# TensorE's order inside one step of a linear-attention and feed-forward kernel: four small-matmul groups and two big ones change places

## The reference

```python
xx = shifted(x) - x;  xk, xv, xr, xg = x + xx * time_maa_{k,v,r,g}
r, k, v = xr @ Wr.T, xk @ Wk.T, xv @ Wv.T          # per head
g = silu(xg @ Wg.T)
def step(state, inp):                              # one chunk of 64 tokens
    att = rc @ kc * w_mat                          # the scores, weighed
    yc = att @ vc + rc @ state * wb                # products with V, products with the state
    new_state = ws * state + kc * wk @ vc          # the state update
out = (normalized(y) * gamma + beta) * g @ Wo.T    # the output projection
x = x + out
x = x + gelu(layernorm(x) @ W0.T + bias0) @ W1.T + bias1
```

## Time and profile before

| | |
|---|---|
| median of three runs | 2102.96 us (2094.62 to 2105.97) |
| the profiled execution | 2098.03 us, its span 2096.2 us |
| TensorE matmuls | 2009.1 us busy, 27206 of them, and as many weight loads |
| VectorE | 1739.2 us busy |
| ScalarE | 1292.4 us busy |
| GpSimd | 317.8 us busy |
| mean granted clock of TensorE | 0.988 of full speed |

### The profile page before, as it was taken

How to read it: one execution, slowest core, us unless ns; L and a number is a source line. 1 busy time by engine, 2 the same in 40 slices (tenths; PEclk the granted TensorE clock), 3 DMA queues, 4 the chain that set the end, 5 groups by cost and what they waited for, 6 DMA issues and landing times.

```text
span 2096.2 us, 64752 instructions
## 1 busy us (share of the span) xinstructions
PE 2009.1 (96%) x27206; PEld 1432.4 (68%) x27206; DVE 1739.2 (83%) x3687; ACT 1292.4 (62%) x2081; POOL 317.8 (15%) x329
## 2 busy tenths in 40 slices
PE   5889999999999999999999999999999999999999
PEld 4777666676766766766766776766776666767666
DVE  7788888888888988888988887888888888888761
ACT  7776565676655667655657765666765656776442
POOL 1011110111111111111111111111111101111110
PEclk8999999999999999999999999999999999999999
DMA  6977786788776788777778877778887867887767
GB/s 212 211 204 237 186 235 211 233 247 237 205 232 200 235 239 237 212 225 215 232 223 242 245 207 210 233 218 245 247 237 192 229 200 244 247 237 205 217 231 254
DMA packets 428979, 471.97 MB, mean 225 GB/s; under 512 B 259600, under 2 KB 309392, under 8 KB 428688
## 3 DMA queue, kind: packets, MB, share of 16 engines
q1 hardware_dynamic: 427056, 467.64, 76.6%
q10 hardware_dynamic: 1632, 0.18, 0.1%
HBM read 316.21 MB, written 25.17 MB: 163 GB/s over the span
## 4 chain that ended last, share of the span: by engine, by line
PE 77%; SPq 5%; DVE 4%; issue 4%; ACT 4%; DMA 4%; POOL 0%; ACTq 0%; DVEq 0%
PE F L1132 19%; PE F L1068 15%; PE B L879 9%; PE B L1040 8%; PE sc L879 7%; PE YT L911 5%; PE YT L879 3%; DMA y<-ygT 3%; PE YT L963 2%; SPq L2026 2%; PE sc L941 2%; PE YT L982 2%; PE F L836 1%; PE YT L1012 1%; SPq L2013 1%
## 5 line engine op out<-in xcount | busy, mean ns | idle before, releaser
L1068 PE MATMUL F<-xT,ring 128*128 128x256 f16 x3840 | 459.0, 276 | 16.6 <-issue 12.1
L1132 PE MATMUL F<-ring,hT 128*128 128x512 f16 x1984 | 467.5, 379 | 0.0
L1068 PEld LDWEIGHTS F<-xT,ring 128*128 128x128 f16 x3840 | 374.0, 99 | 81.4 <-issue 20.3
L1132 PEld LDWEIGHTS F<-ring,hT 128*128 128x128 f16 x1984 | 189.1, 98 | 197.8 <-issue 0.3
L1767 ACT ACTIVATE hT<-F,b,f_rho 128x256 f16<-128x256 f32 x480 | 244.2, 561 | 102.0 <-PE F L1068 102.0
L879 PE MATMUL B<-mix,WT 128*128 128x256 f16 x2304 | 267.5, 273 | 0.1
L879 PEld LDWEIGHTS B<-mix,WT 128*128 128x128 f16 x2304 | 222.6, 98 | 33.4 <-DVE gT L1371 0.3
L276 DVE SCALAR_TENSOR_TENSOR mixf<-dx,maa,xnT 128x256 f32<-128x256 f32 x512 | 238.6, 527 | 0.1
L1724 ACT ACTIVATE Shl<-S 128x256 f16<-128x256 f32 x128 | 53.4, 417 | 257.4 <-PE YT L982 140.4
L1970 POOL TENSOR_TENSOR Shl<-S,Shl 128x256 f16<-128x256 f32 x128 | 89.4, 698 | 756.9 <-ACT Shl L1724 756.9
L1338 DVE TENSOR_TENSOR att<-att 128x512 f16<-128x512 f32 x256 | 166.8, 693 | 39.2 <-ACT att L1718 39.0
(11 more groups left out here) (196 smaller groups left out, 2998.6 us busy)
## 6 DMA issues: line engine op xcount, KB each, us to landing
ring<-w_dram SPq DMA_DIRECT2D x512, 512.0 KB, 4.6
kx<-kT SPq DMA_DIRECT2D x96, 256.0 KB, 3.8
rx<-rT SPq DMA_DIRECT2D x96, 256.0 KB, 4.4
xa<-in_L_attn_x SPq DMA_DIRECT2D x32, 512.0 KB, 7.7
vbd<-vN SPq DMA_DIRECT2D x256, 64.0 KB
x<-in_L_attn_x SPq DMA_DIRECT2D x32, 512.0 KB, 6.3
out<-x SPq DMA_DIRECT2D x31, 512.0 KB, 3.8
w_dram<-ring SPq DMA_DIRECT2D x20, 256.0 KB, 3.5
```

What stands on the lines that cost most here:

```text
L1068: mm = eng.matmul(up_place(f, j)[:, i * BT:(i + 1) * BT], ring[:, use % RING, i, a * C + kk * P:a * C + (kk + 1) * P], xT[:, :, kk, :], st ...
L1132: mm = eng.matmul(F[:, t, :], hT[:, k, rows(t)], ring[:, use % RING, i, a * C:(a + 1) * C], start=(k == 0 and a == 0), stop=(k == NH - 1 a ...
```

## The change

Only TensorE's list changes. The eighth up piece moves from behind the third scores to between the products with V and those with the state; the first half of the output projection moves to right behind the products with the state; then come the third scores and the second tile's state update, which before stood behind the first down piece. The rest of the step stays. No matmul, no semaphore and no wait is added or dropped.

```diff
         if att_n:
             pe_att_v(eng, n, 0)
-            pe_from_state(eng, n, 0)
-            pe_scores(eng, n, 2)
-            pe_prepare(eng, n, "sc2")
         if ff:
             pe_up(eng, n, 7)
+        if att_n:
+            pe_from_state(eng, n, 0)
         if tail:
             pe_Wo(eng, n, 0)
+        if att_n:
+            pe_scores(eng, n, 2)
+            pe_kv(eng, n, 1, n < STEADY)
+            pe_prepare(eng, n, "sc2")
+        if tail:
             pe_prepare(eng, n, "Wo0")
         if ff:
             pe_down(eng, n - 2, 0)
         if att_n:
-            pe_kv(eng, n, 1, n < STEADY)
             pe_scores(eng, n, 3)
```

## The result

| | before | after |
|---|---|---|
| median of seven runs each | 2104.80 us (2094.62 to 2109.18) | 2088.64 us (2083.68 to 2091.96) |
| ratio after to before | | 0.9926, 95% interval 0.9905 to 0.9948 |
| the profiled execution, its span | 2098.03, 2096.2 us | 2091.96, 2090.2 us |
| TensorE on "issue", 250 to 2010 us | 36.5 us in 14 pauses | 10.9 us in 17 pauses |
| undisturbed steps apart | 59.94 us | 60.92 us |

The change makes the kernel 0.7% faster. The two profiled executions differ by only 6.1 us, the medians by 16: that of before (2098.03) was 7 us faster than the median of its kernel, that of after (2091.96) is the slowest of its seven runs.

The account below looks back on a forecast made before the run. TensorE, busy 2009.1 of 2096.2 us, bounds the kernel; pauses and low clock cost 51.8. Span 2096.2 - 43.6 won + 29.2 switches and VectorE wait + 2 late weights = 2083.8; forecast 2086 us, range 2062 to 2107.

Parts of the forecast that it names:

- The pauses are refills of 256 instructions: TensorE's "issue" pauses at the small matmuls: 256 instructions running in less than a refill's 4 to 6 us can stop it.
- What is left is 8.2 us, and 2 for late weights: After the change: 6.5 us of pauses and 1.7 of low clock remain; the eighth piece's late weight loads add 2.
- The first kind: Packets beginning just ahead of or at the V products run out in the projection, 1 to 2 us short: 6.5 us.
- The second kind: Packets beginning in the eighth piece or first state products: 0 to 1 us short, covered by the wait for VectorE.
- Switches, 0.29 us a step: TensorE's added time going between big and small matmul groups, first tile's V products to second's: 0.29 us a step.
- VectorE's residual makes the projection wait 0.70 us: The output projection's second half waits for VectorE's residual, which frees bank B: 0.70 us in every undisturbed step.
- The second wait: Second tile's V products waiting for VectorE's masked update: forecast not to come, but only by 0.1 us.
- 29.5 equal steps: Switches and VectorE's wait, 0.99 us together, counted in each of about 29.5 steps: 29.2 us.
- (a): Rival: VectorE's wait does not come or is small, 20 us less, 2066; chance 0.17.
- (b): Rival: refills move instead of being covered; above 21 us left the change loses, 2106 with ten or more hits; chance 0.10.
- (c): Rival: the change stays within 0.5%, 2092 to 2113 us; chance 0.18.
- (d): Rival: TensorE's pauses are not refills and have another cause; if they stay, 2129 us; chance 0.05.

Follow-up runs that it names:

- e3_lock_on_burst: The kernel before plus 52 redundant score matmuls a step, 40 in step 2, fixing where 256-instruction packets begin, on the burst: 2202.42 us, ratio 1.0465.
- e5_change_lock_off: The kernel after plus 52 redundant score matmuls a step and 28 in step 2, fixing where packets begin: 2119.27 us, ratio 1.0062 to the kernel before.
- after_again: The kernel after, unchanged, measured once more on another chip: 2095.53 us, ratio 0.9939 to the kernel before.
- e2: The kernel after, but with steps 0 and 1 in the old order: 2083.39 us, ratio 0.9903 to the kernel before.
- e6: The kernel after with the third scores moved ahead of the projection's first half: 2095.33 us, ratio 0.9947 to the kernel before.
- e4: The kernel before plus 52 redundant score matmuls a step, 100 in step 2, fixing where packets begin, off the burst: 2059.26 us, ratio 0.9796.
- e7: The kernel after plus 52 redundant score matmuls a step and 100 in step 2: 2095.92 us, ratio 0.9948 to the kernel before.
- e1: The kernel before with only the eighth up piece moved, between the products with V and with the state: 2080.08 us, ratio 0.9887.

## Why the prediction held, point by point

Predicted 2086 us, measured 2088.64; predicted ratio 0.992, measured 0.9926. By its steps:

- **The pauses are refills of 256 instructions.** Shown. I numbered TensorE's instructions in the traces (matmuls, weight loads and its own waits). In the kernel before all 14 pauses on "issue" stand before an instruction whose number is 193 modulo 256, or, where that is a weight load, before its matmul at 194; so do the 27 of e3_lock_on_burst, the 28 of e5_change_lock_off and all 17 of the kernel after, whatever group they fall into; the gaps ahead of L1040 that are waits for VectorE stand at any number. In all 14 of before a packet of the instruction queue starts 2.3 to 2.6 us before TensorE goes on. From the place where the 256 ahead of it began to the end of the pause it is 4.1 to 6.3 us; the prediction had 4 to 6. That figure is no constant, though: it is up to 7.5 us in the kernel after and down to 3.4 in e5, and in e3 another 256 instructions run in 4.04 us in every step with no pause behind them. What stays put is the end, 2.2 to 2.7 us from the packet's start to the matmul after the pause, in all four; what sets when the packet starts no run isolates. The Trainium skill (Runtime: NRT & Kernel Launch, Instruction fetch mechanics) speaks of a store of 2048 instructions for TensorE and also of only two lines of 256, and calls the fetching hidden. The runs agree with the two lines and not with a store that 256 dense instructions cannot empty. Nor was the fetching always hidden: e3 stood 3.0 us a step for it.
- **Pauses and clock cost 51.8 us.** 54.1 were lost in the 28 steps.
- **What is left is 8.2 us, and 2 for late weights.** 13.7 us together against 10.2, 3.5 too little (16.7 in after_again). The places are mostly as foreseen: the largest row is that of the products with the state, then the state update; the 1.7 us in the fourth scores were not named. What they cost shows in the stretch from the V products of the first tile to those of the second, 16.02 us where nothing pauses. The first kind, with a pause in the products with the state (five steps), makes it 5.5 us longer in all, where 6.5 were booked. The second kind, with a pause only in the update or the fourth scores (seven steps), has 4.3 us of pauses but makes it only 1.9 us longer: the wait for the residual behind them covers most of it, as foreseen. Late weights make 1.2 more in one step. The other 5.1 us lie outside this stretch, in part as TensorE's waits for the GELU (2.6 us in 6; before 3.3 in 8), for which the sum had no term. The clock term was right in sign: the mean granted clock between 250 and 2010 us went from 0.99 to 1.00, and not even the one low stretch that was booked followed the short pauses of the kernel after. One of them in the chain of waits of the kernel after, 0.65 us with one matmul of the update left:

```profile
1204.54 0.45 PE YT L1012 x47
1204.99 0.65 issue
1205.64 0.19 PE YT L1012
```

- **Switches, 0.29 us a step.** The timeline after agrees to 0.02 us for every group: the eighth piece 1.85 (booked 1.84), state products 0.51 (0.51), projection 2.69 (2.68), scores ahead of the update 0.32 (0.31), update 0.51 (0.51), down piece 1.83 (1.82), scores 0.38 (0.40).
- **VectorE's residual makes the projection wait 0.70 us.** It waits 0.66 in the step shown (2.39 - 1.73) and 0.73 in the mean of the weight loads. From the first products with V to those of the second tile it is 16.02 us, predicted 15.03 + 0.29 + 0.70 = 16.02. The second wait, which had a margin of 0.1 us, did not come.
- **Blocks 60.9 us apart, "issue" under 10, clock above 0.988, VectorE idle before the third scores.** 60.9, 10.9 (a little over), 0.993 and 0.82 us.
- **The step that failed: 29.5 equal steps.** The sum multiplied 0.99 us by all steps and took no account of what the new order does in steps 0 and 1, where there is no up piece to put between the groups and the update now comes ahead of the weight preparation. They took some 8 us more, as e2 shows. Without that miss the span would have come out below the forecast's own: 2090.2 - 8.4 = 2081.8 against 2083.8.
- **Why the forecast of the median is closer than that of the span.** The sum had 12.4 us of gain in the span; the two profiles show 6.0. The span was 6.4 us above the sum (2090.2 and 2083.8), the median 2.6 above the forecast. The median of before moved up as well when more runs were taken (2104.8), so the gain against it was 16 us, and from the same 2096.2 as the forecast's base it was 6. Within what seven runs of a kernel scatter (8 to 15 us) this can't be told from luck.

The second measurement on another chip, 2095.53, is 9.5 us above the forecast, by its ratio 4 (0.9939 of 2102.96 is 2090). That the first came within 2.6 us is in part luck: the profiled span missed the sum by 6.4, and the median lay 3.3 below the profiled run.

Of the rivals, (a) was wrong, VectorE's wait is there. (b) was half right: pauses moved into the products with the state and the update, but the lost time is 13.7 us, below the 21 from which the change would have lost; e6 shows that this margin hangs on where the projection stands. (c), a change within 0.5%, is out by the first measurement (0.9905 to 0.9948), while the interval of the second (0.9911 to 0.9968) still reaches into it. (d) is excluded by e3 and e4.

## What to carry to other kernels

Where a profile shows TensorE waiting for "issue" inside groups of small matmuls, number its instructions: pauses a multiple of 256 apart are, as here, instruction refills, and in these kernels they came where the 256 instructions ahead took 1.7 to 6 us without the pause (though not at every such place). Put a long group between the short ones, but at a place where it makes no other engine late (the eighth piece did not, the projection ahead of the third scores did), or bring the count of a step to a multiple of 256 and choose the place where the packets begin, which here made the kernel 43 us faster (2102.25 to 2059.26) although it costs 52 useless matmuls a step; the place matters as much as the count, for the same count at another place (e3) made it 100 us slower. And cost a reordering in the first steps by themselves: they have other groups in them than the steady ones.

## What the runs showed of the hardware

- The place of the instructions alone moves this kernel by 143 us, 7%: 2059.3 us or 2202.4 us with the same work in each steady step. An edit that adds or drops instructions of TensorE shifts these places, so that part of its effect can be this and nothing else (e5 and e7: 23 us from 72 redundant matmuls in one early step). All four of these kernels have steps of 7 x 256 instructions; in one with 1688 a step the places walk from step to step anyway, and what a shift does there no run shows.
- How long a refill stops TensorE went with what stands ahead of it: 3.0 us in the third scores (e3), 0.98 us in the fourth, with a down piece ahead of them (e5), 0.38 us in the update behind the projection (e7, 7.2 us in 19).
- In the kernel before 8 of the 14 pauses, of 2.6 to 3.5 us, were followed by a granted clock of 0.51, which is the lower of the two levels, 1.2 GHz; three others as long (2.84, 3.16 and 3.42 us) were not. Pauses of under 1.6 us, in the kernel after and in e5, were followed by none; in e1 one of 1.95 us was. So shorter pauses are worth more than their sum: 25.6 us less pause went with 40.4 us less lost.
